# Cross attention with dense chunks of probabilities, keys and values of both layers made first and kept in DRAM, half the row sums on VectorE

## The reference, cut to what matters

```python
xn = layernorm(x, ln1_w, ln1_b)            # 8 x 512 x 512
yn = layernorm(y, ln2_w, ln2_b)            # 8 x 77 x 384 (layer 1 takes the context as it is)
q = (xn @ Wq).reshape(B, N1, H, hd).transpose(0, 2, 1, 3)
kv = (yn @ Wkv).reshape(B, 77, 2, H, hd)
k, v = kv[:, :, 0].transpose(0, 2, 1, 3), kv[:, :, 1].transpose(0, 2, 1, 3)
attn = softmax(einsum('bhqd,bhkd->bhqk', q, k) * scale, axis=-1)
o = einsum('bhqk,bhkd->bhqd', attn, v).transpose(0, 2, 1, 3).reshape(B, N1, C1)
x = x + (o @ Wproj + bproj)
```

## Time and profile before

| | us |
|---|---|
| median of three runs | 3569.93 |
| profiled execution | 3574.5 |
| its span | 3572.7 |

### The profile page before, as it was taken

One profiled execution on the slowest core, in us unless ns is written; L12 is line 12 of the kernel. 1 busy time (PEld: TensorE's weight loads), 2 busy tenths in 40 slices (PEclk: granted clock), 3 DMA queues, 4 the chain that ended last, 5 costly groups with the idle time before them and its releaser, 6 DMA issues. The chain is left out here.

```text
span 3572.7 us, 43990 instructions
## 1 busy us (share of the span) xinstructions
PE 3265.4 (91%) x14928; PEld 2617.0 (73%) x14928; DVE 1744.5 (49%) x2640; ACT 1689.3 (47%) x4068; POOL 1370.2 (38%) x1487
## 2 busy tenths in 40 slices
PE   4899979999999948999999999768999799999999
PEld 3788867888888835766676667447888588888887
DVE  3566644322223236777777767546666442222221
ACT  2676644222222216666666667436776342222222
POOL 2445421333333326666666566524555211111110
PEclk8999989999999978999999999879999799999999
DMA  3012112111111142334343333231111231111111
GB/s 98 30 65 79 63 59 98 56 48 48 48 48 48 48 127 77 100 99 114 101 108 101 112 99 98 77 97 54 61 58 63 69 99 36 36 36 36 36 36 36
DMA packets 170628, 250.27 MB, mean 70 GB/s; under 512 B 38742, under 2 KB 57382, under 8 KB 170406
## 3 DMA queue, kind: packets, MB, share of 16 engines
q1 hardware_dynamic: 170406, 247.47, 22.7%
HBM read 115.98 MB, written 50.33 MB: 47 GB/s over the span
## 5 line engine op out<-in xcount | busy, mean ns | idle before, releaser
L1065 DVE TENSOR_REDUCE L1sa_nmax<-L1sa_s 128x2 f32<-128x1024 f32 x256 | 310.5, 1213 | 219.9 <-PE L1sa_s L884 219.9
L1157 POOL TENSOR_TENSOR L1sa_El<-L1sa_E,L1sa_Eh 128x1024 fp32r<-128x1024 f32 x128 | 320.8, 2506 | 149.7 <-ACT L1sa_Eh L972 135.5
L468 DVE TENSOR_TENSOR L1ff_gl<-L1ff_gf,L1ff_gh 128x512 fp32r<-128x512 f32 x128 | 96.4, 753 | 470.3 <-ACT L1ff_gh L428 470.3
L468 DVE TENSOR_TENSOR L0ff_gl<-L0ff_gf,L0ff_gh 128x512 fp32r<-128x512 f32 x128 | 97.2, 760 | 439.2 <-ACT L0ff_gh L428 439.2
L414 ACT ACTIVATE L0ff_gf<-L0ff_f,cols 128x512 f32<-128x512 f32 x128 | 88.3, 690 | 449.8 <-PE L0ff_f L94 449.8
L414 ACT ACTIVATE L1ff_gf<-L1ff_f,cols 128x512 f32<-128x512 f32 x128 | 88.3, 690 | 449.8 <-PE L1ff_f L94 449.8
L981 ACT ACTIVATE L1sa_E<-L1sa_st 128x1024 f32<-128x1024 f32 x256 | 260.2, 1016 | 48.0 <-PE L1sa_st L896 47.9
L92 PE MATMUL L1ff_f<-L1ff_hTh,L1ff_Wh 128*128 128x512 f32 x512 | 202.9, 396 | 5.7 <-POOL L1ff_hTl L235 5.7
L92 PE MATMUL L0ff_f<-L0ff_hTh,L0ff_Wh 128*128 128x512 f32 x512 | 202.9, 396 | 5.7 <-POOL L0ff_hTl L235 5.7
L972 ACT ACTIVATE L1sa_Eh<-L1sa_E 128x1024 fp32r<-128x1024 f32 x192 | 200.6, 1045 | 0.1
L93 PE MATMUL L0ff_f<-L0ff_hTh,L0ff_Wl 128*128 128x512 f32 x512 | 200.1, 391 | 0.0
(11 more groups left out here) (306 smaller groups left out, 9053.2 us busy)
## 6 DMA issues: line engine op xcount, KB each, us to landing
L1sa_OLN<-L1sa_osb SPq DMA_DIRECT2D x128, 192.0 KB, 2.7
L0ff_xs<-x SPq DMA_DIRECT2D x64, 256.0 KB, 3.0
L1sa_stack_q<-L1sa_parts_q SPq DMA_DIRECT2D x128, 128.0 KB, 2.6
L1sa_stack_k<-L1sa_parts_k SPq DMA_DIRECT2D x128, 128.0 KB, 2.6
L1ff_xs<-x SPq DMA_DIRECT2D x64, 256.0 KB, 3.6
L0ca_xs<-in_x SPq DMA_DIRECT2D x32, 256.0 KB, 4.0
L0ca_stage<-in_x SPq DMA_DIRECT2D x32, 256.0 KB, 3.5
x<-L0ca_stage SPq DMA_DIRECT2D x32, 256.0 KB, 2.0
```

Source lines behind the costliest of these rows:

```text
L468: nc.vector.tensor_tensor(gl[:, j % 2, :], gf[:, j % 2, :], f32(gh[:, j % 2, :]), ALU.subtract)\
L1065: nc.vector.reduce_max(nmax[:, h % 2, 2 * (n % 2):2 * (n % 2) + 2], s_bank[:, :, :], AX.X, negate=True)\
L1157: nc.gpsimd.tensor_tensor(El[:, n % 2, :], E[:, n % 3, :], f32(Eh[:, n % 2, :]), ALU.subtract)\
```

## The change: what it does

- `context_kv` runs once, ahead of everything, for both layers (layer 1's keys and values first, being the `second` of the names). Its results go to DRAM through buffers `ko` and `vo` of two slots; a slot's next `hi` on ScalarE waits until the slot's store has landed. The query and output weights are split in `cross_attention` itself.
- A batch's keys and values come from DRAM: four DMAs for the keys, six for the values. `place_v` on GpSimd is gone, and the values are placed as the chunks need them.
- The 308 probabilities of a group (4 heads x 77) are transposed in chunks of 128, 128 and 52 instead of four times 77. So a batch has 12 `P_transposed` and 12 `PV` instead of 16, and 12 pairs of `p_hi` and `p_lo`.
- The loop has 24 halves for a batch. `P_transposed(v)` stands at half 2v, `PV(v)` at half 2v + 3, a score tile in two halves of three (tile t + 6 at half floor(1.5 t)), and the 36 quarters of Q, T and O are spread evenly over the halves in the order of `CA_ORDER`. All pieces share the two `pj` banks in turn: a piece waits until the piece two before it is taken out (`bank_free`).
- `SUM_BY`: the row sums of every second tile are made by VectorE from the probabilities; ScalarE's exponentials of these tiles go without the accumulator. GpSimd's `normal` comes a tile later in its order.
- `oTh`/`oTl` have two slots.

In the diff, the first loop over `half` is TensorE's and the second ScalarE's; `row_sum` is VectorE's and runs ahead of `inverse`.

```diff
+        units = [("T", 0, i) for i in range(6)] + [("K", 0, i) for i in range(8)] + [("T", 1, i) for i in range(6)] \
+            + [("V", 0, i) for i in range(B)] + [("K", 1, i) for i in range(8)] + [("V", 1, i) for i in range(B)]
...
+                if kind in "KV":
+                    n = outs[kind].index((kind, layer, i))
+                    stored = (k_stored if kind == "K" else v_stored)[n % 2]
+                    if n >= 2:
+                        act.wait_ge(stored.sem, stored.no(n // 2 - 1))
...
+CHUNK = (P, P, GL - 2 * P)
+CA_STEPS = G * len(CHUNK)
+CA_ORDER = ([("Q", 0, 3)] + [("T", 1, c) for c in range(KT)]
+            + [("O", -1, 0), ("Q", 1, 0), ("O", -1, 1), ("Q", 1, 1), ("O", -1, 2), ("O", -1, 3), ("Q", 1, 2)])
...
+    quarters = [(*u, c) for u in CA_ORDER for c in range(1 if u[0] == "T" else KT)]
+    halves = [[] for _ in range(2 * CA_STEPS)]
+    for i, q in enumerate(quarters):
+        halves[i * 2 * CA_STEPS // len(quarters)].append(q)
...
+        def tile_at(half):
+            t = -(-2 * half // 3)
+            t = t + LEAD if 3 * t // 2 == half else None
+            return None if t is None or t >= B * TILES else divmod(t, TILES)
...
+        SUM_BY = ("act", "dve", "act", "dve")
+        STATS, NORMS, BIAS = (13, 14, 15, 16), (19, 20, 21, 22), (1, 8, 13, 17)
...
+                for j in range(4):
+                    rows = slice(HD * j, HD * (j + 1))
+                    sp.dma_start(f32(Kb[rows, n % 2, :, j, :]), keys[rows, :, n * L:(n + 1) * L])\
+                        .then_inc(e_kb.sem, 16)
...
+                for j, c, row, key, count in head_rows():
+                    sp.dma_start(f32(Vb[row:row + count, n % 2, c, :, HD * j:HD * (j + 1)]),
+                                 values[key:key + count, n, :, HD * j:HD * (j + 1)]).then_inc(e_vb.sem, 16)
...
+            def bank_free(u):
+                kind, b, i = units[u - 2]
+                if kind == "T":
+                    pe.wait_ge(x.e_hf.sem, x.e_hf.at(b, i))
+                elif kind == "Q":
+                    pe.wait_ge(e_ql.sem, e_ql.at(b, i))
                 else:
+                    pe.wait_ge(x.e_res.sem, x.e_res.at(b, i))
...
+                for half in range(HALVES):
+                    tile = tile_at(b * HALVES + half)
+                    if tile:
+                        scores(*tile)
+                    for kind, ahead, i, c in halves[half]:
+                        if exists(b + ahead):
+                            piece(kind, b + ahead, i, c)
+                    if half % 2 == 0:
+                        P_transposed(b, half // 2)
+                    elif half > 1:
+                        PV(b, half // 2 - 1)
...
+                for half in range(HALVES):
+                    if complete(b, half):
+                        o_hi(*complete(b, half))
+                    if half % 2:
+                        p_hi(b, half // 2)
+                    for u in evacs[b * HALVES + half]:
+                        evacuate(*u)
+                    tile = tile_at(b * HALVES + half)
+                    if tile:
+                        exp(*tile)
...
+            def row_sum(b, s):
+                if SUM_BY[s % 4] == "dve":
+                    dve.wait_ge(e_ex.sem, e_ex.at(b, s))
+                    nc.vector.reduce_sum(rsum[:, s // TT, s % TT, :], Pr[:, s // TT, s % TT, :]
+                                         .rearrange("p (j l) -> p j l", j=4), AX.X).then_inc(e_sum.sem, e_sum.unit)
```

More of the change, by code:

```diff
@@ L1395, in cross_attention, with head_rows @@
+def head_rows():
+    pieces = []
+    for j in range(4):
+        at = j * L
+        while at < (j + 1) * L:
+            c = at // P
+            n = min((j + 1) * L, (c + 1) * P) - at
+            pieces.append((j, c, at - c * P, at - j * L, n))
+            at += n
+    return pieces
+def cross_attention(nc, name, cst, x_in, x_out, keys, values, ln_w, ln_b, wq, bq, bv, wo, bo_row):
     with ExitStack() as ctx:
         ph = Phase(nc, ctx, name)
-        Kh, Kl = (ph.sb(n, [P, G, B * L], F32R) for n in ("Kh", "Kl"))
@@ L1658, in _, with complete @@
+            PV(B - 1, CA_STEPS - 1)
+            for t in range(TT):
+                for c in range(KT):
+                    piece("O", B - 1, t, c)
+        def complete(b, half):
+            v = half // 2 - 2
+            if half % 2 or v % C != C - 1:
+                return None
+            return (b, v // C) if v >= 0 else (b - 1, G - 1) if b > 0 else None
         @block.scalar
@@ L1711, in body @@
-            def body(b, par, last):
-                for v in range(H):
-                    if v in OUT and exists(b + OUT[v][0]):
-                        o_hi(b + OUT[v][0], OUT[v][1])
-                    for (ahead, g), steps in Q_STEPS.items():
-                        if steps[-1] == v and exists(b + ahead):
-                            q_hi(b + ahead, g)
-                    if v in T_STEPS and not last:
-                        whole(b + 1, T_STEPS.index(v))
-                    p_hi(b, v)
-                    if has_tile(last, v + LEAD):
-                        exp(*tile(b, v + LEAD))
-                if last:
-                    o_hi(b, G - 1)
@@ new lines, in evacuate, with weights_hi @@
+            def evacuate(kind, b, i):
+                if kind == "T":
+                    whole(b, i)
+                elif kind == "Q":
+                    q_hi(b, i)
+            def weights_hi(first, end):
+                for i in range(first, end):
+                    act.wait_ge(wt.full[i % wt.ns].sem, wt.full[i % wt.ns].at(i // wt.ns, 0))
+                    weight_hi(nc, wt, i).then_inc(wt.hi.sem, wt.hi.unit)
+            cst.wait_cols(act)
+            weights_hi(0, WQ)
+            for u in CA_FIRST:
+                if u == ("Q", 0, 0) and bq is not None:
+                    act.wait_ge(e_bqs.sem, e_bqs.no(0))
+                evacuate(*u)
@@ new lines, in add_output, with finish, weights_lo @@
+                dve.wait_ge(e_out.sem, e_out.at(b, t))
+                add_out(nc, x, pj[no["O", b, t] % 2], t).then_inc(x.e_res.sem, x.e_res.unit)
+            def finish(kind, b, i):
+                if kind == "T":
+                    hi(b, i)
+                elif kind == "Q":
+                    q_lo(b, i)
+                else:
+                    add_output(b, i)
+            def weights_lo(first, end):
+                for i in range(first, end):
+                    dve.wait_ge(wt.hi.sem, wt.hi.no(i))
+                    weight_lo(nc, wt, i).then_inc(wt.lo.sem, wt.lo.unit)
@@ L1936 @@
+            for t in range(TT):
+                bias(B - 1, t)
 class Constants:
```

972 lines of the change are left out of this document (452 added, 520 removed).

## The result

The changed kernel takes 3523.23 us (median of four runs, 3521.93 to 3526.78) against 3569.80 for the kernel before (3568.34 to 3573.32): 46.6 us less, a ratio of 0.987 with a 95% interval of 0.9853 to 0.9887. Forecast were 3509 us and a range of 3480 to 3550. The profiled execution took 3522.49 us, its span 3520.7.

What follows compares the result with a forecast made beforehand. TensorE, busy 249.2 of 254.8 us in middle batches, was taken as the bound. Terms -33 - 30 - 10 + 9 + 3 = -61 us took 3574.5 to 3513.5, less 4.6 for the profiled run: 3509 us, range 3480 to 3550.

Steps and rivals of the forecast that it cites:

- the rivals: Five alternatives: pauses hidden 0.13, clock falls every batch 0.17, half clock throughout pauses 0.06, DRAM loads late 0.05, row-proportional cost 0.03.
- hidden pause: Middle batches: ScalarE and VectorE run earlier, only today's 1.1 us of pauses stay; 28 us more saved, 3481 us; chance 0.13.
- my signs: Trace signs listed beforehand, such as period 48 to 49 us, keys-and-values phase at 98, PV pace not above 0.23.
- Middle batches: Batches 1 to 6, both layers: period falls from 51.0 and 51.6 to 48.5 us, saving 33 us.
- I take a chunk with 128 rows at the price of one with 77: PV on TensorE: duration follows streamed columns, so four fewer P_transposed and PV save 4.6 us a batch.
- Row sums: Middle batches: ScalarE loses 2.9 us a batch, VectorE gains 3.1; off TensorE's path but for the pauses, priced nothing.
- First and last batches: Each layer's first batch saves 6 us and last batch 9 us: 12 + 18 = 30 us in all.
- Keys and values once: The merged phase ahead of both layers ends at 98 us against 108.9 for two phases, saving 10 us.
- Prologue: Query and output weights split there: +2 us before the first Q, +2.5 between exponentials; 9 us for both layers.
- Clock: TensorE at half clock after the new pauses, at most 3.4 us, in one batch in ten or so: 3 us.
- my second rival: The clock falls in every batch: 12 x 3.4 = 41 us back, 3547 us; chance 0.17.
- Loads from DRAM: Each batch's keys and values, ten DMAs, are asked for half to a whole batch before use; priced nothing.

Runs made afterwards that it cites:

- experiment 1: Changed kernel with the third chunk's products reading 128, 64 or 72 rows instead of 52 (three kernels): 3497.24, 3523.5 and 3499.5 us.
- experiment 4: Changed kernel with all row sums made by ScalarE's accumulation, none on VectorE: 3534.22 us, ratio 0.9909 to the kernel before.
- experiments 1, 2, 4 and 5: Changed kernel edited; 2: bank evacuations ahead of probability splits, 3507.20 us; 5, two kernels: value weights split earlier, 3517.1 us, or four store slots, 3517.5 us.

## Why the prediction was right, and where its terms were off

The result lies in the range, on the side of the forecast, 14 us above it. In the trace none of the rivals happened: clock 1.00 in all middle batches, no wait of PV for a load, no hidden pause. Some of my signs did come out against me: the period is 49.7, not 48 to 49, the third chunk's products have a pace above 0.23 us, and the phase of keys and values ends at 105.0, not 98. And luck had a part: the first batches and the last ones missed by 5.4 and 5.5 us in opposite directions, and the medians are 5 us further apart than the stages add up to.

*Middle batches, forecast -33, measured -18.3.* Pauses 1.93 + 1.64 against 1.9 + 1.5: the chain by which I placed the second transpose behind q_lo held to a few hundredths. From the start of P_transposed(1) at 253.79, q_lo begins at 2.05 us (forecast 2.04), the second transpose at 2.78 (2.80) and the first output quarter at 7.26 (7.22). What failed is "I take a chunk with 128 rows at the price of one with 77", read as the price of every chunk. The work of a batch was to be 44.7 us; it is 49.7 - 3.6 = 46.1, and the difference is the third chunk with its 52 rows, 1.56 a batch by experiment 1. The period missed by 1.2 us, 49.7 against 48.5: these 1.5, less the 0.3 that I had added for small pauses and that are not there. In twelve batches that is the 15 us by which this term was too large.

*Row sums, forecast nothing.* Measured 0.3 to 0.4 us a batch through the second pause (experiment 4). "Neither is on TensorE's path but for what the pauses hold" was the place. Its price was hidden in the other term: the pause of 1.5 us was worked out with exponentials without accumulator, 4 x 0.21.

*First and last batches, forecast -12 and -18, measured -6.6 and -23.5.* In the last TensorE is busy 33.1 of 36.1 us, as worked out (32.0, and 37 with waits); I had applied layer 0's 46.8 to layer 1, whose last batch took 49.2. In the first, 3 us a layer instead of 6, I left out the two pauses that I had charged to the middle batches, and the row switches. Spaced transposes take it from 47.0 to 43.7 us in layer 0, products of all rows to 45.6.

*Keys and values once, forecast -10, measured -5.1.* The pause for the value weights came as said: forecast 47, measured 49.57. After it I counted TensorE's 44 us plus a few, and let the stores pass for free, though I had charged them to layer 1's keys. With two slots they paced ScalarE: 18.4 us of waits on the values' stores and 9.6 on those of layer 0's keys. From the first value product to the first load it took 55.4 us, not 51. Four slots and the weights ahead end the phase at 84.8.

```profile
49.57 0.68 PE L92 MATMUL kv_bank<-kv_wvh,kv_cTh 128*77 128x512 f32 x1 [10.49 <-DVE kv_wvl L151]
```

*Prologue, forecast +9, measured +11.7.* The two terms, +2 before the first query and +2.5 between the exponentials, measured 1.9 and 2.5 in layer 0. Missing was GpSimd, which has a larger value buffer to fill (128 x 6144 instead of twice 128 x 2048) and the inverse square root behind it. From the first load to the first transpose of tokens it is 12.9 us instead of 11.6:

```profile
105.04 4.21 POOL L1946 MEMSET L0ca_Kb<- 128x4928 f32 x1
109.18 5.23 POOL L1947 MEMSET L0ca_Vb<- 128x6144 f32 x1
114.50 0.19 POOL L207 TENSOR_SCALAR L0ca_ve<-L0ca_mv 128x4 f32<-128x4 f32 x1
```

The statistics were ready at 111.63 (VectorE's four aggregates start at 111.27 and take 0.36 together).

*Clock, forecast +3.* The middle batches ran at 1.00; the first ones at 0.89, where the earlier trace rows have 0.93 and layer 1 had 0.86. No net cost is seen in this trace. The mechanism of my second rival does occur, only rarely and small. In the traces of the eight kernels that keep both pauses (this one and those of experiments 1, 2, 4 and 5), 7 of the 48 middle batches of layer 1, and none of layer 0's 48, hold one stretch of 3.4 us at half clock (1.2 of 2.4 GHz), and take 1.1 to 1.6 us more each. The last full batch with 64 rows, 51.1 us instead of 49.7:

```profile
2679.80:2730.90 51.10, 47.93 (x245) 38.33 (x244) 30.69 (x69) 33.15 (x122) 21.04 (x24) 0.97 0.17 48
```

The traces of the five kernels with spaced transposes have none. I had guessed one batch in ten at 3.4 us.

*Loads from DRAM, forecast nothing.* No product of the middle batches waited for one. From the table of DMA issues after (count, KB, median us to landing):

```profile
L0ca_Kb<-L_keys SPq DMA_DIRECT2D x32, 77.0 KB, 2.6
```

The keys from DRAM land in 2.6 us where the copies inside SBUF took 2.0, and the cover of a whole batch hid it. That is the direction of the rule that the prediction cites from the Trainium skill (DMA: Bandwidth & Descriptors, "Why small descriptors are slow (HBM only)"). But each of these DMAs carries 77 KB instead of 38.5, so the rows don't tell the source's part from the size's. For the values, with their pieces of 128 bytes, the trace gives no landing time.

## What to carry to other kernels

Price a matmul by its columns only as long as its neighbours are of its kind; here products of 52 or 64 rows between products of 128 cost extra, products of 72 or 77 did not. So a small remainder chunk between full ones is cheaper with zeros in its empty rows. Pauses that an order itself makes could be worked out here to 0.15 us from start-to-start distances, and the better cure was distance between pieces that share two banks (36 to 40 us), not a change of priority (12 to 16 us). When stores leave through two slots, count their landing as a stage of the pipeline, and look for the second wait behind the first: each cure alone gave 6.0 and 9.6 of the some 20 us that both gave.

## What the runs showed of the hardware that was not expected

- TensorE, 512 columns at full clock: a switch between 52 or 64 rows and 128 costs about 0.1 us for each of four matmuls at the chunk, 1.56 us for four chunks; 72 or 128 rows cost nothing.
- VectorE's `tensor_scalar` on 128 x 512 in SBUF, four of them: 1.92 us with GpSimd idle, 6.78 beside a fill of 5.24 us on GpSimd, 5.41 of them for the first. `bn_stats` took 0.68 to 0.70 us each beside GpSimd's fills and 0.69 beside ScalarE's: those were not held.
- ScalarE fills 128 x 6144 with zeros in 5.32 us, GpSimd in 5.23.
- In kernels with two pauses of 1 to 2 us in each middle batch, 7 of layer 1's 48 such batches hold a stretch of 3.4 us at half clock, which costs 1.1 to 1.6 us; layer 0's 48 hold none.
